# Between two attentions of one network: normalisation split by image, weight products moved, and products of ones at other waits

## Chip, cores and metric

The kernel runs on one core of a Trainium2 chip. The metric is the device time of one execution in microseconds (us); the median over the runs is compared. The engines are TensorE (PE), VectorE (DVE), ScalarE (ACT), GpSimd (POOL) and SyncE (SP), each with a queue of its own that runs in program order and waits on semaphores.

## What is computed

The input is x, two images of 128 channels and 32 x 32 places. Three blocks follow one another.

```python
# 1: attention over 7 x 7 neighbourhoods, on group-normed x
q, k, v = (einsum('bchw,oc->bohw', gn(x), w) + b for each of wq, wk, wv)
frac = einsum('bchw,bcphw->bhwp', q, unfold(k)); attn = softmax(where(frac != 0, frac, -inf))
out = einsum('bhwp,bcphw->bchw', attn, unfold(v))
out = (out - mean over batch and places) * rsqrt(var + 1e-5) * gamma + beta
x = x + relu(out)
# 2: attention over tokens, 8 heads, on layer-normed tokens t (2, 1024, 128)
q, k, v = reshape(ln(t) @ Wqkv + bqkv, (3, b, n, d, h))
attn = softmax(score over queries, axis=1); av = einsum('bnnh,bnqh->bnqh', attn, v)   # the diagonal
t = t + reshape(av) @ W0 + b0
# 3: a mixture of experts, the best 2 of 8 per image, on layer-normed tokens
t = t + ffn(ln(t))            # router on the mean token, gelu, a layer norm at its end
```

All matrix products whose precision matters are made of a rounded part and a remainder (hi and lo), three products in place of one.

## The kernel before, in words

Channels lie on the 128 partitions, the 2048 tokens (image 0, then image 1) on the free axis, in four chunks of 512. PSUM has eight banks of 512 float32; `bank(n)` is one of them and `slot(n)` two neighbouring ones, so the token attention has four slots. All work is written as one list per engine, in program order.

**First attention.** 16 tiles of 128 queries in `CONV_STEPS` steps, software pipelined: scores of tile s, transposes of tile s-2 (L865) into `out_bank`, a copy `probsT` by ACT (L547), products with the values of tile s-3 (L874), and an eviction to `conv_e` by ACT (L562). PE makes products of ones (`keep_warm(bank, count)`, L751: bf16, 128 x 512, result unused) in some of its waits here and later on. DVE then takes batch statistics (L1257, L1316), ACT the square root (L585), DVE scale and bias (L1319 to L1322), ACT six Relus over thirds of an image (L591), and DVE adds x (L1332) and gives x1.

**The fold.** The values' part of the token attention uses W0 folded into the weights: `fold` = 24 blocks of 128 x 128, made from transposed blocks of Wqkv and from W0. PE transposes the 24 blocks (L887), ACT copies them out (L574), PE multiplies (`fold_products`, L905) into six banks, ACT copies those to `fold` (L580). The bias columns go through W0 too (L894), are split into three bf16 parts by POOL (L441, L444), transposed by PE (L956) and copied by DVE (L1362).

**Normalisation of tokens.** `channel_means` (L910, float32 products with 1/128, two instructions for a chunk), `centre` by DVE (L1337), `square` by ACT (L598), `variances` (L918, eight instructions for a chunk), one `root` by ACT (L604), one reciprocal by DVE (L1343), `spread` (L929, eight instructions for a chunk) and the product of both by DVE (L1350) give xn. `LN_PARTS` says which chunks share one root; for the first of the three normalisations all four do. `centred` lies in the same memory as `queries_full`'s two chunks and two more.

**Token attention.** 16 units (image, head), each with one projection of queries and of keys (L981) and eight score tiles (L997 to L999), taken by DVE (`maximum`: L1380 and L1385) and ACT (the exponential with its sum, L644). `JOBS` lists projections, score tiles and one transposition in order; job g lies in slot g % 4 and PE waits in `slot_free(g)` until job g-4 has been taken. A projection of unit u+1 comes behind score tile 0 of unit u; ACT takes hi parts (L622, L634), DVE and POOL the remainders (L1370, L449). The tokens that the reshape gives to image 0's queries are 0 to 341, to its keys 682 to 1024, and to the values 1365 to 2047.

```python
JOBS = [("queries", 0, 0), ("keys", 0, 0)] + [job for u in range(UNITS) for job in unit_jobs(u)]
def job_slot(job):
    return JOB_AT[job] % SLOTS
```

After it come the values (L1047, L1056), the second normalisation, the router, and the experts: `hidden(n)` (L1127 to L1129) and `outputs(n)` (L1142 to L1144) in turn on PE, Gelu on ACT (L724, L731), then the last normalisation and the stores.

Inputs come on SP's and ACT's DMA queues: x in two orders, then Wqkv, W0, x and the experts' weights.

## Time and profile before

| what | value |
|---|---|
| median of 3 runs | 435.48 us (434.71 to 436.42) |
| the profiled execution | 432.75 us |
| its span, first to last instruction | 431.0 us |
| mean granted clock of TensorE | 0.987 of full |
| PE busy | 408.3 us, 95% |
| DVE busy | 322.6 us, 75% |
| ACT busy | 300.2 us, 70% |
| POOL busy | 69.1 us, 16% |

The times of the trace are those of the one profiled execution, so sums are made against its 432.75 us. A busy share is a mean over stages: the last eviction of the first attention starts at 57.60, the first score tile at 90.51, and the last at about 321 us. PE's clock has two levels, 1.2 and 2.4 GHz, shown as 0.50 and 1.00.

### The profile page before, as it was taken

The numbers are of one execution on the slowest core, as the hardware profiler recorded it, in microseconds if no ns is written. First come the engines' busy times: TensorE is split into PE (matmuls) and PEld (weight loads), VectorE is DVE, ScalarE is ACT, GpSimd is POOL, SyncE is SP. The second block draws the span as 40 slices with busy tenths as digits, with TensorE's granted clock in tenths as the row PEclk, the third lists the DMA queues.
The fourth block names the chain that finished last, engine by engine and source line by source line (L and its number), as shares of the span: only waits on it lengthen the run. The fifth ranks groups of instructions, "written<-read, shape, count | busy, mean of one in ns | idle before, by whom it ended". The sixth has DMA issues, their size and how long they took to land.

```text
span 431.0 us, 5798 instructions
## 1 busy us (share of the span) xinstructions
PE 408.3 (95%) x2003; PEld 312.6 (73%) x2007; DVE 322.6 (75%) x707; ACT 300.2 (70%) x579; POOL 69.1 (16%) x72
## 2 busy tenths in 40 slices
PE   7899779999999999999998999999999999879996
PEld 3578766958888888888876888888867666537763
DVE  3788853349888988898899789888997565567654
ACT  1567694459999999999979899999981101555740
POOL 8400011024210221022102112211200000440000
PEclk9999998999999999999999999999999999998998
DMA  7950000000000000000000000000000000000002
GB/s 269 361 144 1 2 2 0 2 0 3 0 1 2 0 2 1 1 2 0 0 2 2 2 0 0 2 1 1 2 0 2 0 0 2 0 2 2 0 2 97
DMA packets 3887, 9.73 MB, mean 23 GB/s; under 512 B 530, under 2 KB 1682, under 8 KB 3730
## 3 DMA queue, kind: packets, MB, share of 16 engines
q1 hardware_dynamic: 3426, 8.39, 5.5%
q10 hardware_dynamic: 432, 0.97, 0.6%
q8 instruction: 16, 0.26, 0.2%
q14 instruction: 13, 0.11, 0.1%
HBM read 8.31 MB, written 1.05 MB: 22 GB/s over the span
## 4 chain that ended last, share of the span: by engine, by line
PE 77%; DVE 14%; ACT 4%; issue 3%; POOLq 0%; POOL 0%; DVEq 0%; ACTq 0%
PE ps L981 12%; PE ps L997 11%; PE ps L999 11%; PE ps L998 11%; PE ps L1056 7%; DVE nmax_all L1380 6%; PE ps L918 3%; PE ps L929 3%; PE ps L751 2%; PE ps L910 2%; PE ps L874 2%; PE ps L1047 1%; PE ps L905 1%; PE ps L849 1%; PE ps L1142 1%
## 5 line engine op out<-in xcount | busy, mean ns | idle before, releaser
L1380 DVE TENSOR_REDUCE nmax_all<-ps 128x1 f32<-128x1024 f32 x128 | 156.8, 1225 | 5.7 <-PE ps L999 3.8
L644 ACT ACTIVATE exps<-ps,nmax_all 128x1024 bf16<-128x1024 f32 x128 | 143.5, 1132 | 13.9 <-DVE diag_all L1385 13.9
L997 PE MATMUL ps<-qT_hi,kT_hi 128*128 128x512 f32 x256 | 104.1, 407 | 2.2 <-ACT exps L644 1.0
L999 PE MATMUL ps<-qT_hi,kT_lo 128*128 128x512 f32 x256 | 99.8, 390 | 0.0
L998 PE MATMUL ps<-qT_lo,kT_hi 128*128 128x512 f32 x256 | 99.7, 389 | 0.0
L449 POOL TENSOR_TENSOR qT_lo<-xq,qT_hi 128x1024 fp32r<-128x1024 f32 x16 | 38.5, 2405 | 198.9 <-ACT xq L634 198.9
L997 PEld LDWEIGHTS ps<-qT_hi,kT_hi 128*128 128x128 f32 x256 | 48.1, 188 | 14.9 <-ACT exps L644 2.0
L981 PE MATMUL ps<-xn,wqkv 128*128 128x342 f32 (+3 forms) x256 | 58.2, 379 | 0.0
L998 PEld LDWEIGHTS ps<-qT_lo,kT_hi 128*128 128x128 f32 x256 | 48.1, 188 | 10.8
L999 PEld LDWEIGHTS ps<-qT_hi,kT_lo 128*128 128x128 f32 x256 | 48.1, 188 | 10.3
L981 PEld LDWEIGHTS ps<-xn,wqkv 128*128 128x128 f32 x256 | 42.6, 189 | 10.9 <-ACT exps L644 0.5
L1370 DVE SCALAR_TENSOR_TENSOR kT_lo<-ps,cols,kT_hi 128x341 fp32r<-128x341 f32 (+1 forms) x48 | 24.5, 567 | 30.8 <-ACT kT_hi L622 30.8
L1385 DVE CUSTOM_DVE_ANT_0 diag_junk<-ps,ident 128x128 f32<-128x128 f32 x128 | 36.0, 281 | 0.0
L1056 PE MATMUL ps<-xs,fold 128*128 128x342 f32 (+3 forms) x128 | 30.6, 381 | 0.6 <-DVE xs L1446 0.6
L622 ACT ACTIVATE kT_hi<-ps,cols 128x341 fp32r<-128x341 f32 (+1 forms) x48 | 22.7, 546 | 10.5 <-PE ps L981 10.5
L598 ACT ACTIVATE squares<-xq 128x512 f32<-128x512 f32 x12 | 7.5, 629 | 29.9 <-DVE xq L1337 29.9
L1446 DVE TENSOR_TENSOR xs<-xv,ps 128x1024 f32<-128x1024 f32 x16 | 19.4, 1220 | 11.2 <-PE ps L1047 11.2
L644 ACT ACTIVATION_READ_ACCUMULATOR exps<-ps,nmax_all 128x1 f32 x128 | 27.7, 217 | 0.0
L751 PE MATMUL ps<-filler 128*128 128x512 bf16 x84 | 23.8, 427 | 2.7 <-DVE filler L1189 1.5
L1056 PEld LDWEIGHTS ps<-xs,fold 128*128 128x128 f32 x128 | 21.1, 189 | 6.6 <-DVE xs L1446 1.1
L634 ACT ACTIVATE qT_hi<-ps,bqkv_q 128x341 fp32r<-128x341 f32 (+1 forms) x48 | 23.0, 570 | 1.4 <-PE ps L981 1.4
L634 ACT ACTIVATE xq<-ps,bqkv_q 128x341 f32<-128x341 f32 (+1 forms) x48 | 23.3, 594 | 0.0
(200 smaller groups left out, 516.4 us busy)
## 6 DMA issues: line engine op xcount, KB each, us to landing
wqkv<-laid_qkv_weights SPq DMA_DIRECT2D x1, 1536.0 KB, 6.2
xq<-laid_x_queries SPq DMA_DIRECT2D x2, 512.0 KB, 6.8
xk<-laid_x_keys SPq DMA_DIRECT2D x2, 512.0 KB, 8.3
x<-in_x SPq DMA_DIRECT2D x1, 1024.0 KB, 9.3
w<-in_L_ffn_W SPq DMA_DIRECT2D x1, 1024.0 KB
out<-conv_e SPq DMA_DIRECT2D x4, 256.0 KB, 2.0
band_sb<-laid_band ACTq DMA_DIRECT2D x1, 724.0 KB, 10.0
w<-in_L_attn_W SPq DMA_DIRECT2D x1, 512.0 KB, 7.2
```

The costliest lines, as they stand in the source:

```text
L449: g.tensor_tensor(qT_lo[:, u % 2, :], queries_full, qT_hi[:, u % 2, :].bitcast(F32), ALU.subtract)\
L634: a.activation(dst[:, lo:hi], slot(job_slot(("queries", u, 0)), lo, hi), ACT.Identity, bias=bqkv_q[:, j, h:h + 1], scale=SCORE_SCALE).then ...
L644: a.activation(exps[:, n % 2, :], slot(job_slot(("score", u, n))), ACT.Exp, bias=nmax_all[:, col:col + 1], accum_out=sum_all[:, col:col + ...
L751: mm(bank(n), filler[:, 0:P], filler[:, :], start=True, stop=True)
L981: last = mm(slot(job_slot((kind, u, 0)), at, at + n), wqkv[:, h, j, :], xn[:, tok:tok + n], start=True, stop=True)
L997: mm(tgt, keys_hi, qT_hi[:, u % 2, at], start=True, stop=False)
L998: mm(tgt, keys_hi, qT_lo[:, u % 2, at], start=False, stop=False)
L999: last = mm(tgt, keys_lo, qT_hi[:, u % 2, at], start=False, stop=True)
L1056: last = mm(slot(SUMS_SLOT[b], at, at + n), fold[:, h, j, :], xs[:, u % 2, at:at + n], start=False, stop=False, skip_group_check=True)
L1370: inst = v.scalar_tensor_tensor(kT_lo[:, u % 2, lo:hi], slot(job_slot(("keys", u, 0)), lo, hi), bqkv[:, j, h:h + 1], kT_hi[:, u % 2, lo:hi ...
L1380: v.tensor_reduce(nmax_all[:, col:col + 1], slot(place), AX_X, ALU.max, negate=True)\
L1385: v.tensor_tensor_reduce(out=diag_junk[:, :], in0=slot(place, tile * P, (tile + 1) * P), in1=ident[:, :], scale=1.0, scalar=0.0, op0=ALU.m ...
```

## The change

- **By DMA.** Transposed blocks of Wqkv come as an input of their own (`qkv_weights_T`, 1.5 MB) into `wvT`, in memory that is used otherwise only during the token attention. The 24 transposes and their six copies are gone. The new transfer is issued behind Wqkv and ahead of W0, x and the rest.
- **The fold's place.** The bias products come first behind the first attention's last product, in bank 0, then all six banks of fold products (banks 6, 7, 1, 2, 6, 7), ahead of the channel means. ACT copies banks 0 and 1 of them before the square root of the batch statistics, and the others behind the Relus.
- **Batch statistics.** The addition of 1e-5 goes into the root's bias, a product and a subtraction become one instruction. The Sqrt table is loaded in step 16 of the first attention's 19 and not behind it. ACT makes the Relus of image 0 only; POOL scales and shifts the thirds of image 1, and DVE takes their maximum with 0 in the same instruction that adds x.
- **Normalisation in two parts**, chunks 0 and 1 (one root) and chunks 2 and 3. Only chunks 0 and 1 are finished before the first projection. The spread of chunks 2 and 3 and their two products become a job in unit 1 ahead of score tile 4, the transposition of the bias parts one in unit 2 ahead of tile 4. With two more jobs, the slots and banks of the value stage, the second normalisation and the router are renumbered. POOL's copy of the values' tokens goes one unit later.
- **Products of ones.** Removed: one ahead of the first group statistics, one behind them. Added or moved: 11 at four waits behind the fold; 3, 5 and 7 (5, 5 and 5 before) around the first evictions; 12 between the first hidden products and the first outputs; 3 ahead of the last three spreads; and 4 and 4 with a wait between where 14 stood ahead of the last spread.

```diff
-        FOLD_AT = (5, 7, 6, 5, 7, 6)
+        FOLD_AT = (6, 7, 1, 2, 6, 7)
+        VB_BANK = 0
...
-        LN_PARTS = [((0, 1, 2, 3),), ((0, 1), (2, 3)), ((0, 1, 2), (3,))]
+        LN_PARTS = [((0, 1), (2, 3)), ((0, 1), (2, 3)), ((0, 1, 2), (3,))]
...
+        EXTRA_AT = {"spread": (1, 4), "biases": (2, 4), "turned": (HEADS + 1, 4)}
...
+            sp.dma_start(wvT[:, :, :, :], t["qkv_weights_T"]).then_inc(wvT_in, 16)
...
+            pool.wait_ge(bn_aff, 1)
+            pool.wait_ge(folded, 2)
+            for lo, hi, _ in THIRDS:
+                third = conv_e[:, 1, lo * RUN:hi * RUN]
+                g.tensor_scalar(third, third, st[:, 30:31], st[:, 31:32], ALU.mult, ALU.add).then_inc(bn_scaled, 1)
...
                     take_job(*STEP_JOB[s])
-
-            load_table(ACT.Sqrt)
...
-            take_transposed(0, 2)
-
-            act.wait_ge(bn_eps, 1)
-            a.activation(st[:, 26:27], st[:, 26:27], ACT.Sqrt).then_inc(bn_root, 1)
-            take_transposed(2, 4)
+                if s == CONV_TILES:
+                    load_table(ACT.Sqrt)
...
+            take_folded(0)
+            take_folded(1)
+            act.wait_ge(bn_stats, 1)
+            a.activation(st[:, 26:27], st[:, 25:26], ACT.Sqrt, bias=norm_eps[:, :]).then_inc(bn_root, 1)
             act.wait_ge(bn_aff, 1)
             act.wait_ge(folded, 2)
-            for b in range(2):
-                for lo, hi, _ in THIRDS:
-                    a.activation(conv_e[:, b, lo * RUN:hi * RUN], conv_e[:, b, lo * RUN:hi * RUN], ACT.Relu,
-                                 scale=st[:, 30:31], bias=st[:, 31:32]).then_inc(bn_relu, 1)
-            take_transposed(4, FOLD_BANKS)
+            for lo, hi, _ in THIRDS:
+                third = conv_e[:, 0, lo * RUN:hi * RUN]
+                a.activation(third, third, ACT.Relu, scale=st[:, 30:31], bias=st[:, 31:32]).then_inc(bn_relu, 1)
+            for n in range(2, FOLD_BANKS):
+                take_folded(n)
...
-            for c in range(4):
-                square(0, c)
-            take_folded(0, 2)
             act.wait_ge(norm_consts, 3)
-            root(0, 0, 4)
+            square(0, 0)
+            square(0, 1)
+            root(0, 0, 7)
+            square(0, 2)
+            square(0, 3)
+            root(0, 1, 0)
             load_table(ACT.Exp)
-            take_folded(2, FOLD_BANKS)
...
             pe.wait_ge(xq_in[0], 16)
-            keep_warm(7, 4)
+            keep_warm(7, 3)
...
+            pe.wait_ge(wvT_in, 16)
+            for job in (("q", 2 * CHUNKS - 1), ("v", 2 * CHUNKS - 1)):
+                taken(*job)
+            for n in range(FOLD_BANKS):
+                fold_products(n)
+            for signal, count, times in ((bn_root, 1, 3), (bn_aff, 1, 3), (bn_relu, 1, 3), (bn_relu, 2, 2)):
+                pe.wait_ge(signal, count)
+                keep_warm(5, times)
...
+            pe.wait_ge(cx_sb, CONV_TILES)
+            pe.wait_ge(x1_ready, 3)
+            channel_means(0, 0, x1, "mean", 3)
+            channel_means(0, 1, x1, "mean", 4)
+            pe.wait_ge(x1_ready, 6)
+            channel_means(0, 2, x1, "mean", 5)
+            pe.wait_ge(f_m_sb, 5)
+            channel_means(0, 3, x1, "mean", 6)
+            pe.wait_ge(f_m_sb, 6)
+            variances(0, 0, 7, 0)
+            variances(0, 0, 7, 1)
+            pe.wait_ge(vb_sb, 1)
+            variances(0, 1, 0, 2)
+            variances(0, 1, 0, 3)
+            pe.wait_ge(LN[0]["centred"], 2)
+            spread(0, 0, 3)
+            spread(0, 1, 4)
+            pe.wait_ge(LN[0]["sqrt"], 2)
...
+            def spread_rest(n):
+
+                pe.wait_ge(LN[0]["rstd"], 2)
+                for i in range(8, 16):
+                    last = mm(bank(n + i // 4 - 2, i % 4 * P, (i % 4 + 1) * P), row_sel[:, i, :], rstd[:, 1, :],
+                              start=True, stop=True)
+                last.then_inc(job_ps, 1)
...
+                    if (u, n) == EXTRA_AT["spread"]:
+                        dve.wait_ge(job_ps, JOB_AT["spread", 0, 0] + 1)
+                        place = 2 * job_slot(("spread", 0, 0))
+                        for c in (2, 3):
+                            at = slice(c * 512, (c + 1) * 512)
+                            v.tensor_tensor(xn[:, at], centred[:, at], bank(place + c - 2), ALU.mult)\
+                                .then_inc(LN[0]["out"], 1)
...
             hidden(0)
             hidden(1)
+            keep_warm(7, 8)
+            pe.wait_ge(h_sb, 1)
+            keep_warm(7, 4)
...
+            keep_warm(5, 3)
             for c in range(3):
                 spread(2, c, 1 + c)
             pe.wait_ge(u_ready, 4)
             variances(2, 1, 6, 3)
-            keep_warm(5, 14)
+            keep_warm(5, 4)
+            pe.wait_ge(LN[2]["sqrt"], 2)
+            keep_warm(5, 4)
             spread(2, 3, 4)
```

## Rows read from the trace of the kernel before

**Rows 1.** Chain that ended last: start us, us, engine and line.

```profile
1.52 6.39 PE ps L751 x16
...
61.04 1.68 PE ps L894 x16
62.72 1.60 issue
64.32 5.37 PE ps L910 x8
...
90.51 0.50 PE ps L997
```

**Rows 2.** Timeline in the second normalisation: start us, us, engine, line, operation, count.

```profile
365.18 1.88 PE L910 MATMUL ps<-t,mean_w 128*128 128x512 f32 x4
...
367.71 1.92 PE L918 MATMUL ps<-squares,mean_window 128*16 128x128 f32 x16 [0.65 <-ACT squares L598]
```

**Rows 3.** Timeline of PE, first expert outputs; in brackets the idle time before.

```profile
388.84 0.47 PE L1142 MATMUL ps<-hid_hi,w_hi 128*128 128x512 f32 x1 [2.03 <-ACT hid_hi L731]
...
393.26 0.40 PE L1142 MATMUL ps<-hid_hi,w_hi 128*128 128x512 f32 x1
```

**Rows 4.** Windows of PE: from:to, length, busy (count), granted clock, DMA, GB/s.

```profile
65.50:66.00 0.50, 0.50 (x2) 0.50 0.00 0
...
389.50:390.00 0.50, 0.50 (x3) 0.50 0.00 0
...
420.50:421.00 0.50, 0.50 (x4) 0.50 0.19 74
```

**Rows 5.** Timeline of PE in the first attention.

```profile
48.78 0.41 PE L865 MATMUL ps<-ident,probs 128*128 128x128 f32 x2 [1.95 <-DVE probs L1294]
```

**Rows 6.** Chain that ended last, projections in the token attention.

```profile
92.16 3.46 PE ps L981 x16
106.53 3.46 PE ps L981 x16
```

**Rows 7.** Group of the page: busy us, mean ns of one, idle before.

```profile
L1380 DVE TENSOR_REDUCE nmax_all<-ps 128x1 f32<-128x1024 f32 x128 | 156.8, 1225 | 5.7 <-PE ps L999 3.8
```

**Rows 8.** Timeline of ACT at the end of the first attention.

```profile
55.71 0.48 ACT L562 ACTIVATE conv_e<-ps,conv_b 128x128 f32<-128x128 f32 x1 [0.19 <-PE ps L874]
56.04 0.48 ACT L547 COPY probsT<-ps 128x384 f32<-128x384 f32 x1
...
57.60 0.48 ACT L562 ACTIVATE conv_e<-ps,conv_b 128x128 f32<-128x128 f32 x1 [0.41 <-PE ps L874]
58.10 1.28 ACT L497 ACT_TABLE_LOAD   x1
...
59.51 1.06 ACT L574 COPY xv<-ps 128x512 f32<-128x512 f32 x2
60.45 0.21 ACT L585 ACTIVATE st<-st 128x1 f32<-128x1 f32 x1
...
61.50 3.50 ACT L591 ACTIVATE conv_e<-conv_e,st 128x352 f32<-128x352 f32 x6
```

**Rows 9.** Timeline of PE in the first normalisation: fold, first projections.

```profile
69.53 1.95 PE L905 MATMUL ps<-w,xv 128*128 128x128 f32 x16
...
82.80 3.68 PE L981 MATMUL ps<-xn,wqkv 128*128 128x342 f32 x16
```

**Rows 10.** Timeline of POOL at the start.

```profile
15.96 0.48 POOL L430 TENSOR_SCALAR conv_ws<-conv_wT,st 128x256 f32<-128x256 f32 x1 [0.92 <-DVE st L1206]
```

**Rows 11.** Timeline at the end of the kernel.

```profile
422.42 3.55 PE L751 MATMUL ps<-filler 128*128 128x512 bf16 x13 [0.33 <-issue]
422.68 0.93 DVE L1343 RECIPROCAL rstd<-rstd 16x128 f32<-16x128 f32 x1
...
427.09 0.69 DVE L1350 TENSOR_TENSOR xq<-xq,ps 128x512 f32<-128x512 f32 x1 [3.48 <-PE ps L929]
```

**Rows 12.** Slices of the page, 40 over the span: busy tenths of the DMA engines.

```profile
DMA  7950000000000000000000000000000000000002
```

224 lines of the change are left out of this document (109 added, 115 removed).

## Prediction

> **What bounds the kernel now.** I read the chain that ended last first, because TensorE (PE) is busy nearly everywhere and the busy share alone says little. Three places matter. Between the attentions [rows 1] the chain is PE: products of bias columns from 61.04, 1.60 us in which PE does nothing, four channel means from 64.32 that take 5.37 us, then folds, variances and spreads up to the first projection, and the first score tile at 90.51. The reader should see that the means are 8 instructions of 0.67 us each, while the same 512 column means later take 0.47 (four in 1.88) [rows 2]. The windows by clock say why: at 65.5 the granted clock is 0.50, the 1.2 GHz level, right after the idle 1.60 us. The same level stands at 389.5, after 2.03 us of idle PE [rows 3], and at 420.5 near the end [rows 4]. But 1.95 us of idle PE before 48.78 in the first attention was followed by no fall [rows 5], so idle time alone does not decide it.
>
> The long stretch of score tiles is PE's too: 14.37 us from one unit's projections to the next [rows 6], of which 3.46 are projections and 8 tiles take 1.36 each. VectorE (DVE) takes 1.23 for a maximum [rows 7], and the picking of the diagonal fills the tile's time up, so it keeps step in the tiles and catches up only during the projections: 3.46 less the key remainders over 1024 elements, which I put at 1.5 (an estimate: a maximum reads as many in 1.23, and these are three starts), so 1.9 us per unit.
>
> **Start.** One product of ones fewer before the group statistics. The chain begins with these 16 products [rows 1], not with the statistics, so one product comes off the path: 512 columns at 2.4 GHz, 0.213 us. The other one removed lies ahead of a wait for scaled weights: nothing. Sum: -0.2.
>
> **The Sqrt table.** Its load moves from behind the last eviction of the first attention to two steps earlier, behind the eviction at 55.71. There ScalarE (ACT) has no free time: the copy of the last transposed tile started at 56.04 [rows 8], overlapping that eviction, which ends at 56.19. The load costs 1.41 from its start to that of the next instruction (58.10 to 59.51), so the copy starts at about 57.60, 1.56 late, and with it PE's last three products, the last eviction and the statistics. Before, that load lay beside the statistics, so nothing is gained for it. The Trainium skill ("ScalarE: Activation LUTs", What ACT_TABLE_LOAD costs) adds a drain of about 1.38 us to the 1.28 of each load; the trace shows 1.28 and the next instruction 0.13 behind it. By that rule the step would be 1.25 dearer; I take the row.
>
> **PE's queue from there.** The 24 transposes and their six copies go, since the transposed weights come by DMA. PE ended the last product by 57.60, where its eviction starts [rows 8]; now 59.15. The 16 bias instructions take 1.7 to 1.85 (1.68 in the chain, 62.72 the end) [rows 1] and end at about 60.9. The six fold banks follow at once: 24 blocks of two instructions. Sixteen took 1.95 with the tail of the last [rows 9], 0.1175 a step, so 48 take 5.64, to 66.6. Banks 6 and 7 are used twice, for which ACT must have copied the first two; it has. Then 11 products of ones at four waits, 0.213 each: 2.35 us, to 68.9. They are not free unless the waits are late, so check them. The square root waits behind the copy of the second bank on ACT: that bank ends at 62.8 and its copy takes 0.53 (two in 1.06), so the root starts at 63.4. From the root's start to the first Relu were 1.05 with four steps of DVE; with three, 0.9: 64.3 instead of 61.50 [rows 8], 2.8 later although the statistics are ready 1.56 late only. Three Relus of 0.58 (six in 3.50) end at 66.0, the sums of image 0 at 66.5 and, three of about 0.45 more, of image 1 at 67.9. All four waits are thus over before PE comes to the products of ones, and PE's queue sets the means: 68.9.
>
> Image 1's thirds go to GpSimd (POOL). The nearest row is 0.48 for 256 elements [rows 10]; a third has up to 352, so 0.6 to 0.7 each, ready at 66.4, needed by the third mean at 70.6. Cover 4 us.
>
> **Normalisation.** Four means at full clock, 0.86 each, end at 72.4. From a mean's start to the variance of its square are 2.53 [rows 2], long over by then, so PE goes on with the variances of chunks 0 and 1, 16 steps, to 74.3. ACT takes the root before square 2: with 0.4 for the root and 0.7 for the square (an estimate: 2.53 less a mean, shared by centring and square, leaves 0.8) PE idles 1.1, then variances 2 and 3 to 77.3. Two spreads, 1.9, end at 79.2. The reciprocal (0.93) [rows 11] is long done. Queries need chunk 0 only, keys chunk 1. So the projection starts at 79.2 instead of 82.80 [rows 9], and from projection to first score (90.51) is the same chain of evictions, 7.7 us: first score at 86.9. The products of ones in it lie beside evictions. Between the attentions: -3.6.
>
> **What is given back.** The spread of chunks 2 and 3 (16 instructions, 1.88) and the three bias transposes (three steps, 0.35) stand now among the score tiles, where PE is the bound: +2.2. DVE gets two products of 0.69 (as in [rows 11]) behind a maximum, and one small copy. The spread's own slot is freed by those two; the score tile four jobs on waits some 0.3 for it: +0.3. The rest of DVE's delay is under the 1.9 of the next projections. Sum: +2.5.
>
> **Feed-forward.** Twelve products of ones now fill the idle 2.03. They take 2.56, start where PE fell idle (386.65 by the step, 388.84 less 2.03 less the tail) and end at 389.2, 0.35 past the old start. Twelve products from 388.84 to 393.26 took 4.42 [rows 3]; at full clock twelve take 2.76 (a score tile's six take 1.36, and a little for the join). Gain 1.66 less 0.35 = 1.3, of which I take 1.2, since the Gelu chain is close behind.
>
> **End.** Before, 14 products of ones stand between the last variance and the last spread, part of them at half clock: 422.42 to 425.97 [rows 11]. The reciprocal starts at 422.68, behind the third chunk's output on DVE, and is done at 423.6. With eight split by a wait the spread starts at 423.7 when the clock stays up, and the last normalisation at 424.85 for 427.09: -2.2. When the clock still falls, the eight end near 424.6: -1.3. The three new ones before the spreads lie where PE waits for a reciprocal. I take 2.1, near the full-clock end, since these three fill idle time right ahead of the fall.
>
> **DMA.** The 1.5 MB more is queued on SyncE ahead of W0, x and the feed-forward weights. All inputs are over within the first three slices of 10.8 us, where the DMA share of a slice falls from 9 tenths to 5 and then to nothing [rows 12]; the 1.5 MB, a sixth more than what was moved in all, reach about half a slice further, and the transposed weights, W0 and x are first used at 59 or later. Nothing. The value stage only exchanges banks: nothing.
>
> **Sum.** -0.2 - 3.6 + 2.5 - 1.2 - 2.1 = -4.6. The profiled execution took 432.75 (span 431.0): 428.15, span 426.4. The median of the runs is 2.73 above the profiled time, so 435.48 - 4.6 = 430.9.
>
> **Rivals.**
> *The clock falls in the fold.* The table load opens 1.56 us of idle PE, after which come six short products and 1.85 us of three-column products, the make-up that preceded the fall at 65.5 [rows 1, 4]; against it stands the gap before 48.78 without one [rows 5]. One stretch at half clock cost 1.66 in the feed-forward [rows 3]; 1.7: 432.6. Chance 0.27.
> *The products of ones don't hold the clock* in the feed-forward (then they only cost 0.35, so 1.55 worse) or at the end (0.8 worse): up to 433.2. For it: the fall at 420.5 stood behind spreads with no long idle time. Chance 0.14.
> *The table load is hidden*, since the copy is not as tight as in this execution: 1.56 better, 429.3. Against it: the start of 56.04 lies inside the previous eviction [rows 8]. Chance 0.08.
> *POOL holds image 1 (the other side).* If a third took over 1.9 us instead of 0.6, the means of image 1 wait; at 4.2 us each the gain of 4.6 and 2.2 more are gone: over 437.7. It decides from 3.4 us on. The row of 0.48 for 256 elements speaks against it. The Trainium skill ("SBUF — State Buffer", Who interferes with whom) lets a DVE instruction with two SBUF inputs and a GpSimd one that reads SBUF block each other for a whole instruction. By that rule POOL would wait for up to three sums of 0.45, some 1.4 more, still covered; no row here shows such a pair. Chance 0.03.
> *DVE's delay in the attention is not absorbed*: another 1.4, 432.3. Chance 0.06, in no sum of the others.
>
> **Numbers.** My forecast 0.42. Range 428.6 (table hidden, a little more) to 433.5 (half clock, or ones without effect). About 0.5% (2.2 us) is what a measurement of this kernel can tell from no change. Faster by more needs under 433.3: forecast, hidden load, most of the two clock rivals, 0.84; within, 0.12; slower, 0.04.
>
> **What would show it.** The last copy of probsT 1.5 after the eviction before it. The four means right behind the products of ones, at 0.43 per instruction and clock 1.00. The first projection near 79, the first score near 87. One unit longer by 2.2 and 0.3, another by only 0.35. Clock 1.00 at 389 to 393. No PE gap of more than 0.9 before the last spread. It would be wrong if PE waited for a sum of image 1, if the half clock stood in 58 to 66, or if score tiles waited for slots for more than 0.5 us.

## The result and the profile after

The change makes the kernel faster: a median of 430.55 us over 20 runs (428.15 to 435.86) beside 434.25 (432.76 to 436.42, 20 runs) of the kernel before, ratio 0.9909, 95% interval 0.9884 to 0.9934. The ratio leaves out four runs of the changed kernel (435.09 to 435.86) that lie more than 1.5% above its fastest; the medians keep them. The forecast of 430.9 stood on a median of 435.48 from 3 runs; over 20 runs that median is 434.25, so the medians fell by 3.70 and not by 4.6, and the near hit on 430.55 is in part luck. The profiled execution took 428.15 (span 426.4, mean granted clock 0.999), 4.60 less than the one of before.

Stage by stage, each cut at the first instruction of a step, from the two profiled executions:

| stretch, us | before | after | difference | predicted |
|---|---|---|---|---|
| start of the span to the first score product of the first attention | 15.78 | 14.62 | -1.16 | -0.2 |
| from there to the first score tile of the second | 74.73 | 70.88 | -3.85 | -3.6 |
| from there to the first `xs` of the values | 231.86 | 235.48 | +3.62 | +2.5 |
| to the first hidden product | 61.37 | 61.38 | 0.0 | 0 |
| to the start of the last outputs | 29.53 | 28.32 | -1.21 | -1.2 |
| to the last normalisation | 13.82 | 11.80 | -2.02 | -2.1 |

The sum came out as predicted, -4.6, but because two terms missed in opposite directions: the start is 1.0 better and the attention 1.1 worse than the prediction had them. The start's 1.0 is luck of this pair of executions, as the last part of this section shows.

**Between the attentions.** The chain that ended last; it answers to [rows 1] and the fold and projections of [rows 9]:

```profile
57.05 0.91 PE ps L871 x6
57.96 1.68 PE ps L884 x16
59.64 5.46 PE ps L892 x48
65.10 2.37 PE ps L748 x11
67.48 3.43 PE ps L906 x8
70.91 1.86 PE ps L914 x16
...
73.82 1.91 PE ps L914 x16
75.73 1.98 PE ps L925 x16
...
77.79 1.98 PE ps L973 x8
...
85.50 0.50 PE ps L989
```

The 1.60 us of idle PE and the slow means are gone. PE goes from the last products of the first attention through the bias products (L884), the 48 fold instructions (L892), 11 products of ones (L748) and the means (L906) without a wait, and the eight mean instructions take 3.43 for 5.37.

The timeline of ACT at the end of the first attention, beside [rows 8]:

```profile
54.55 0.48 ACT L563 ACTIVATE conv_e<-ps,conv_b 128x128 f32<-128x128 f32 x1 [0.19 <-PE ps L871]
55.04 1.28 ACT L498 ACT_TABLE_LOAD   x1
...
56.45 0.46 ACT L548 COPY probsT<-ps 128x384 f32<-128x384 f32 x1
```

and PE behind it:

```profile
57.05 0.91 PE L871 MATMUL ps<-probsT,vtok 128*128 128x128 f32 x6 [1.55 <-ACT probsT L548]
```

The load starts right behind an eviction, and the last transposed tile is copied 1.41 later; PE waits 1.55 for it.

The batch normalisation and the first sums, on three engines:

```profile
63.10 1.80 ACT L585 ACTIVATE conv_e<-conv_e,st 128x352 f32<-128x352 f32 x3 [0.75 <-DVE st L1347]
63.17 3.11 POOL L438 TENSOR_SCALAR conv_e<-conv_e,st 128x352 f32<-128x352 f32 x3 [46.89 <-DVE st L1347]
63.88 1.63 DVE L1360 TENSOR_TENSOR x<-x,conv_e 128x352 f32<-128x352 f32 x3 [0.72 <-ACT conv_e L585]
...
65.43 1.62 DVE L1363 SCALAR_TENSOR_TENSOR x<-conv_e,x 128x352 f32<-128x352 f32 x3
```

POOL's thirds take 1.04 each in the mean (one by one 0.63, 0.95 and 1.55), and DVE's sums of image 1 follow 1.55 behind those of image 0. All are over at 67.05, before the first mean at 67.48.

**In the attention.** Chain, projections, and the spread's job (L1008), beside [rows 6]:

```profile
87.15 3.46 PE ps L973 x16
...
101.52 3.46 PE ps L973 x16
...
109.08 1.98 PE ps L1008 x16
...
126.74 0.50 PE ps L989
...
133.85 3.46 PE ps L973 x16
```

From the projections at 101.52 to those at 133.85 (two units, the middle ones start at 118.22) are 32.33 us where two plain units take 28.74: 3.59 more, all that the attention lost. In the second of these units PE waits 0.53 for an exponential (L641) ahead of the tile at 126.74.

**Feed-forward and end.** Timelines of PE, beside [rows 3] and [rows 11]:

```profile
385.26 2.76 PE L748 MATMUL ps<-filler 128*128 128x512 bf16 x12
387.68 0.58 PE L1161 MATMUL ps<-hid_hi,w_hi 128*128 128x512 f32 x1
...
418.80 1.90 PE L748 MATMUL ps<-filler 128*128 128x512 bf16 x8
...
421.29 1.15 PE L925 MATMUL ps<-rstd,row_sel 16*128 16x128 f32 x8 [0.59 <-DVE rstd L1373]
```

The outputs follow the products of ones without a gap. At the end the reciprocal starts at 420.30 and takes 0.93, as in [rows 11], but the spread waits 0.59 for it and not for a row of fourteen products. Windows of PE where the clock was at half in [rows 4] (length, busy, count, granted clock):

```profile
65.50:66.00 0.50, 0.50 (x4) 1.00 0.00 0
389.50:390.00 0.50, 0.50 (x4) 1.00 0.12 33
420.50:421.00 0.50, 0.20 (x1) 1.00 0.13 45
```

**The start.** Timeline of DVE and POOL of the kernel before:

```profile
9.21 3.56 POOL L416 TENSOR_SCALAR_AFFINE_SELECT head_sel<-head_sel 72x1024 bf16<-72x1024 bf16 x3
...
9.71 1.90 DVE L1224 TENSOR_SCALAR conv_ws<-conv_wT,st 128x128 f32<-128x128 f32 x3
```

and after:

```profile
8.93 1.51 DVE L1249 TENSOR_SCALAR conv_ws<-conv_wT,st 128x128 f32<-128x128 f32 x3
9.19 3.64 POOL L412 TENSOR_SCALAR_AFFINE_SELECT head_sel<-head_sel 72x1024 bf16<-72x1024 bf16 x3
```

DVE's three scalings of the convolution's weights started 0.78 earlier and ended 1.17 earlier (10.44 for 11.61). The three selects take 1.09 to 1.18 each and start 1.23 to 1.32 apart. After, the scalings end 0.08 behind POOL's first select (10.36), before, 0.08 behind its second (11.53). The prediction did not look at this pair.

The 0.78 is not the removed product alone. At the start the products of ones begin 0.43 us apart, and at some moment they go over to 0.21. That moment differs between executions, and with it the time at which PE comes to the statistics. Two of the experiments below, e9 and e10, have the changed kernel's instructions up to here. Their timelines, e9:

```profile
1.52 5.14 PE L748 MATMUL ps<-filler 128*128 128x512 bf16 x15 [1.52 <-DVE filler L1211]
...
8.56 0.83 DVE L1246 TENSOR_SCALAR conv_ws<-conv_wT,st 128x128 f32<-128x128 f32 x3
```

and e10:

```profile
1.52 6.35 PE L748 MATMUL ps<-filler 128*128 128x512 bf16 x15 [1.52 <-DVE filler L1211]
...
9.66 1.92 DVE L1246 TENSOR_SCALAR conv_ws<-conv_wT,st 128x128 f32<-128x128 f32 x3
```

The same 15 products take 5.14, 5.62 (changed kernel) and 6.35 us; the 16 of before took 6.39 [rows 1]. Over all profiled executions that have the selects at the start:

| profiled executions | first scaling starts (first select: 9.19 to 9.21) | statistics of image 1 start |
|---|---|---|
| e2, e3, e6, e8, e9 | 8.56 to 8.67 | 10.05 to 10.37 |
| changed kernel, e7 | 8.93, 8.89 | 10.49, 10.45 |
| e1 (16 products of ones) | 9.23 | 11.64 |
| e4, e5, e10 | 9.34, 9.61, 9.66 | 11.64 |
| kernel before (16 products of ones) | 9.71 | 11.66 |

An execution whose scalings start ahead of the select starts the statistics of image 1 some 1.2 us earlier, and three of the ten executions with 15 products did not get that far.

### The profile page after: what moved, and what is told of

The parts are those of the page before. It is cut to its first block, busy times and chain, and to the rows that moved or that the text cites. A ratio compares the mean times of both kernels' runs of the same rounds, so it can differ in the third digit from the quotient of the medians.

```text
span 426.4 us, 5791 instructions
## 1 busy us (share of the span) xinstructions
PE 405.3 (95%) x2001; PEld 308.8 (72%) x2001; DVE 323.1 (76%) x707; ACT 295.5 (69%) x571; POOL 71.4 (17%) x75
## 4 chain that ended last, share of the span: by engine, by line
PE 73%; DVE 17%; ACT 6%; issue 3%; POOLq 0%; POOL 0%; DVEq 0%; ACTq 0%
PE ps L973 11%; PE ps L989 10%; PE ps L991 10%; PE ps L990 10%; DVE nmax_all L1414 7%; PE ps L1075 7%; PE ps L748 3%; PE ps L914 2%; PE ps L906 2%; PE ps L925 2%; PE ps L871 2%; PE ps L1066 1%; PE ps L846 1%; PE ps L892 1%; ACT exps L641 1%
## 5 line engine op out<-in xcount | busy, mean ns | idle before, releaser
L641 ACT ACTIVATE exps<-ps,nmax_all 128x1024 bf16<-128x1024 f32 x128 | 143.3, 1132 | 18.5 <-DVE diag_all L1419 17.9
L748 PE MATMUL ps<-filler 128*128 128x512 bf16 x106 | 27.9, 405 | 2.2 <-DVE filler L1214 1.5
L641 ACT ACTIVATION_READ_ACCUMULATOR exps<-ps,nmax_all 128x1 f32 x128 | 27.9, 218 | 0.0
```

What stands on the lines that cost most here:

```text
L641: a.activation(exps[:, n % 2, :], slot(job_slot(("score", u, n))), ACT.Exp, bias=nmax_all[:, col:col + 1], accum_out=sum_all[:, col:col + ...
L748: mm(bank(n), filler[:, 0:P], filler[:, :], start=True, stop=True)
```

## The experiments

Each profiled execution has its own stretches at half clock (of about 4 us at the fold, 4 to 11 us in the router between 366 and 390, and at the end), so a step is compared with the same step at the same clock.

**e1: the start put back.**

```diff
-            keep_warm(7, 3)
+            keep_warm(7, 4)
...
-            keep_warm(7, 2)
+            keep_warm(7, 3)
```

> The changed kernel with the two products of ones at the start restored (4 and 3 in place of 3 and 2). In the two traces everything behind the start was 1.16 us earlier with the change, where the prediction had 0.2. Theory: the two products are worth that 1.16, the first by its own 0.4 (it runs at the low start rate) and the rest by what lies beside it on GpSimd, so the first score product of the first attention goes back from 14.6 to about 15.8. Rival: the 0.2 of the prediction is right and the rest is the landing of the first input, which differs from execution to execution (DVE began its first statistics at 5.47 before and at 5.01 after); then that product starts at about 14.8 to 15.2, whatever the products of ones.

Measured (one run, 433.91): the first score product at 15.76 for 14.62 (15.78 before). In this execution the fold fell to half clock, 7.09 us for 5.46; less that, the stretch up to the second attention is the changed kernel's to 0.01 (72.51 less 1.63, and 70.88). The timeline of e1:

```profile
9.19 3.55 POOL L412 TENSOR_SCALAR_AFFINE_SELECT head_sel<-head_sel 72x1024 bf16<-72x1024 bf16 x3
9.23 2.36 DVE L1249 TENSOR_SCALAR conv_ws<-conv_wT,st 128x128 f32<-128x128 f32 x3
```

DVE starts 0.04 behind POOL and not 0.26 ahead, and its three take 2.36: the first ends with the first select (10.36), the second in the gap before the next, the third with the second select (11.59). The first product at 15.76 is what the theory had, but one run does not show that the products of ones are its cause: e4, e5 and e10 lose the same race without them. In e1's own execution one product fewer, 0.21, would have put the scalings at 9.02, ahead of the select (an estimate); in that of the kernel before, at 9.50, it would not. The rival, a later landing of the input, fell: DVE's first statistics start at 4.89 here for 5.01.

**e11: POOL's selects away from DVE's scalings.** The memset and the selects of `head_sel` go behind the remainder of the first queries; PE waits for them before the first broadcast.

```diff
-            step(g.memset(head_sel[:, :, :], 0.0))
-            for part in range(3):
...
+            pool.wait_ge(ws_ready[0], 3)
             g.memset(conv_e[:, :, :], 0.0).then_inc(zeroed, 1)
...
                 queries_remainder(u)
+                if u == 0:
+                    step(g.memset(head_sel[:, :, :], 0.0))
```

> The changed kernel with GpSimd's memset and its three selects of head_sel moved from the start to behind the remainder of the first queries, and the memset of conv_e behind VectorE's three scalings of the convolution's weights: GpSimd is idle while VectorE scales. Theory (VectorE's scalings are held by GpSimd's selects): the three take 0.72 us in all for 1.51, each in 0.24, and the first score product is at 13.8 for 14.62. Rival (the scalings wait for something else, or the second image's landing is late next): the three still take 1.5, or they take 0.72 and the first score product stays at 14.6. The selects, now at some 82 to 87 us, may hold VectorE there by up to 1 us ahead of the first exponentials.

Measured: 428.85 (4 runs), ratio 0.9859 (0.9816 to 0.9902). Its timeline:

```profile
8.61 0.68 DVE L1250 TENSOR_SCALAR conv_ws<-conv_wT,st 128x128 f32<-128x128 f32 x3
...
10.25 1.29 DVE L1222 BATCH_NORM_STATS2 bn<-xq 128x6 f32<-128x512 f32 x2 [0.53 <-DMA xq<-laid_x_queries]
```

With POOL's selects away, three scalings take 0.68 for 1.51, 1.90 and 2.36: it was POOL that held them. The first score product comes at 14.39, only 0.23 earlier, because now the landing of the second half of `xq` at 10.23 is late: DVE's statistics wait 0.53 for it. Both halves of the expectation are thus answered, the hold by the theory, the gain by the rival; in the changed kernel the statistics start at 10.49, so its start has 0.25 left to give, and kernels that won the race with the selects in place (e3, e6) are at 14.27 and 14.19. What the move buys is that the race cannot be lost.

**e2: the table load back behind the last eviction.**

```diff
-                if s == CONV_TILES:
-                    load_table(ACT.Sqrt)
+
+            load_table(ACT.Sqrt)
```

> The changed kernel with the Sqrt table loaded behind the loop of the first attention again. Theory (the prediction's term): the load in step 16 holds the copy of the last transposed tile and with it PE's whole queue by 1.56 us, so without it the gap of 1.55 us in PE before the last products goes, and the first score tile of the token attention starts 1.5 us earlier, 84.0 for 85.5 where the start is the same; the time falls by 1.5 us. Rival: the load then lies in the way of the fold's first copies and of the root, and the gain is taken back there: under 0.3 us, or a loss.

Measured: 428.40 (4 runs), ratio 0.9878 (0.9816 to 0.9940). From the first score product to the second attention 69.35 for 70.88: 1.53 less. The bias products start at 56.28 for 57.96, without a gap ahead of PE's last products, and all behind them follows in the same distances (fold 5.46, products of ones 2.37, means 3.43), since PE's queue sets the time. The early load bought nothing and cost what the prediction had for it (1.56).

**e3: without the 11 products of ones behind the fold.**

```diff
-            for signal, count, times in ((bn_root, 1, 3), (bn_aff, 1, 3), (bn_relu, 1, 3), (bn_relu, 2, 2)):
-                pe.wait_ge(signal, count)
-                keep_warm(5, times)
```

> The changed kernel without the 11 products of ones between the fold and the channel means. Theory (the prediction's term): all four waits are over when PE comes to them, so they cost 2.3 us and hold nothing; the sums of image 0 are ready at 65.5 and those of image 1 at 67.05, the fold ends at 65.1, so the means start at 65.5 for 67.5 and PE then waits for the second image's sums once, a few tenths: the first score tile comes 1.7 to 2.0 us earlier. Rival: the products keep the clock up, and without them the means run at 1.2 GHz as in the kernel before: then the gain of 2 is eaten by 1.7 and the time stays the same within 0.5 us.

Measured: 429.96 (10 runs), ratio 0.9870 (0.9834 to 0.9905); the interval overlaps the changed kernel's. The profiled execution has the fold at half clock, as e1's has; against e1 the stretch is 71.17 for 72.51, 1.34 less and not 2.37, since PE now waits for image 0's sums. Its chain:

```profile
65.40 1.65 DVE x L1357 x3
67.05 0.14 issue
67.18 3.67 PE ps L903 x8
```

The means ran at full clock behind that wait, so these 11 products did not hold the clock here. Of their 2.37 us 1.34 come back in this execution. The sums are late in it because the root stands behind ACT's copy of the second fold bank, which the half clock delays (its copy starts at 63.09, the root at 63.57). At whole clock, as in the changed kernel's trace, image 0's sums are over at 65.51, so 1.97 would come back (an estimate: 67.48 less 65.51); and with the root ahead of those copies 2.19 do (e9 against e2, 67.16 for 69.35, both at whole clock there).

**e4: the spread's job ahead of the next unit's projections, at tile 1 of unit 1.**

```diff
-        EXTRA_AT = {"spread": (1, 4), "biases": (2, 4), "turned": (HEADS + 1, 4)}
+        EXTRA_AT = {"spread": (1, 1), "biases": (2, 4), "turned": (HEADS + 1, 4)}
```

and in the order of jobs it stands ahead of the keys and queries, with DVE's two products ahead of the tile's maximum.

> The changed kernel with the spread of chunks 2 and 3 as the job ahead of the projections in unit 1 (behind score tile 0), and its two products on DVE ahead of the key remainders. Theory: of the 3.6 us that units 1 and 2 take more than two others, 1.98 and 0.35 are PE's own work and 1.26 come from DVE, whose two products of 0.69 stand where it keeps step with PE; behind score tile 0 DVE waits 1.7 us for key remainders anyway, so they are free there, and units 1 and 2 together take 31.1 us in place of 32.3, the time falls by 1.2. Rival: the 1.26 are a wait for the slot that the spread holds, wherever it stands: units 1 and 2 keep 32.3 and the time is the same.

Measured: 436.24 (10 runs), ratio 0.9947 (0.9902 to 0.9993). From the first score tile of the second attention to `xs` 235.97 for 235.48. The theory fell: DVE has the projections to catch up in, and the attention still loses as much. (The rest of the 10.0 us that this profiled execution takes more than the changed kernel's is the lost race at the start, 1.2, and half clock: 2.8 more at the start, 2.5 up to the second attention, 2.1 in the router, 0.9 at the end.) The timeline of PE shows where:

```profile
107.93 2.05 PE L1010 MATMUL ps<-rstd,row_sel 16*128 16x128 f32 x16
...
114.51 0.50 PE L991 MATMUL ps<-qT_hi,kT_hi 128*128 128x512 f32 x1 [0.87 <-ACT exps L643]
```

The wait is not one for DVE. The tile behind the projections (109.91, 3.73 long) waits for an exponential on ACT, which stands behind the eviction of the keys. That speaks for the rival, a cost of the extra job wherever it stands; e7 and e10 test it.

**e7: the second half's spread and products in the wait for the first keys.** The job in the attention stays, with one product of ones of 128 columns in it.

```diff
             pe.wait_ge(LN[0]["centred"], 4)
-            keep_warm(5, 3)
-            pe.wait_ge(q_full, 2)
-            keep_warm(5, 5)
+            spread(0, 2, 5)
+            spread(0, 3, 6)
             pe.wait_ge(k_hi, 2)
-            keep_warm(5, 7)
+            keep_warm(7, 7)
+            pe.wait_ge(LN[0]["out"], 3)
...
+            normalise(0, 2, 5, xn)
             keys_remainder(0)
+            normalise(0, 3, 6, xn)
...
-                for i in range(8, 16):
-                    last = mm(bank(n + i // 4 - 2, i % 4 * P, (i % 4 + 1) * P), row_sel[:, i, :], rstd[:, 1, :],
-                              start=True, stop=True)
+                mm(bank(n, 0, P), filler[:, 0:P], filler[:, 0:P], start=True, stop=True).then_inc(job_ps, 1)
```

> The changed kernel with the spread of chunks 2 and 3 in the place of 8 products of ones behind the first two projections, where PE waits for evictions, and DVE's two products on both sides of the first key remainders; the job in unit 1 is one product of ones without a use. Theory: both are free there, so the first score tile stays at 70.9 us behind the first attention's first score and the stretch from it to the values falls from 235.5 to 232.4 (the bias job with its slot and copy is left), 3 us faster. Rival: the excess comes from the two extra jobs in the ring of four slots and not from the work in them: then it falls by PE's 1.9 only.

Measured: 429.75 (4 runs), ratio 0.9873 (0.9780 to 0.9966). The first score tile comes at 85.53 (85.50): the work in the wait is free. The attention is 233.41 for 235.48: 2.07 less, and not the 3 of the theory: the rival held. The spread's own time (1.98) came back, with 0.09 beside it for all of DVE's two products, and 1.55 of the loss stayed with two jobs, of which one holds a single short product and the other the three transposes.

**e9: all moves together.** e7 and the bias transposes in the same wait (their job empty too), the table load of e2, no products of ones behind the fold (e3), and the root of the batch statistics ahead of the copies of the first two fold banks.

```diff
+            act.wait_ge(bn_stats, 1)
+            a.activation(st[:, 26:27], st[:, 25:26], ACT.Sqrt, bias=norm_eps[:, :]).then_inc(bn_root, 1)
             take_folded(0)
             take_folded(1)
-            act.wait_ge(bn_stats, 1)
-            a.activation(st[:, 26:27], st[:, 25:26], ACT.Sqrt, bias=norm_eps[:, :]).then_inc(bn_root, 1)
```

> All that the runs point to: as the one before, with the bias transposes in that wait as well, the Sqrt table loaded behind the loop, the root ahead of the fold's first two copies and no products of ones ahead of the means. Theory: 1.5 for the table, 2 for the products, 3.3 for the work taken out of the score tiles: the first score tile at 81.5 to 82.5, the values' first product at 314, 6.5 us faster than the changed kernel in the same state of the clock. Rival: once the fold's end comes earlier, the sums of the second image are late next, GpSimd's three thirds of 1.04 us each behind the root, and PE falls idle ahead of the means so that the clock falls there: 3 to 4 us faster only.

Measured: 423.09 (4 runs), ratio 0.9737 (0.9683 to 0.9790). First score tile at 81.67, where the theory had it, and the rival did not come: PE does not wait ahead of the means, and the clock stays whole there. From the first score product to `xs` e9 is 5.8 shorter than the changed kernel and not 6.5, since the attention keeps 233.43: emptying the second job changed nothing (233.41 in e7). Its timeline of PE at the first of the two jobs:

```profile
104.86 0.39 PE L988 MATMUL ps<-qT_hi,kT_lo 128*128 128x512 f32 x1
105.09 0.23 PE L1003 MATMUL ps<-filler 128*128 128x128 bf16 x1
105.72 0.50 PE L986 MATMUL ps<-qT_hi,kT_hi 128*128 128x512 f32 x1 [0.40 <-ACT exps L641]
```

One product of 128 columns, then 0.40 us of wait for an exponential; the unit, from the projections at 97.52 to those at 112.66, is 15.14 long for 14.37. The job has taken a place in the ring of four, so the tile behind it needs the slot of the tile three before it, not four.

**e10: e9 without the two jobs.** 161 jobs, slots and banks of the later stages as in the kernel before.

```diff
-        EXTRA_AT = {"spread": (1, 4), "biases": (2, 4), "turned": (HEADS + 1, 4)}
+        EXTRA_AT = {"turned": (HEADS + 1, 4)}
-        SUMS_SLOT = (3, 2)
+        SUMS_SLOT = (1, 0)
```

> The kernel that has all moves ahead of the attention (e9), and without its two extra jobs, which there held one product of ones each: 161 jobs in the ring of four as before the change, with the slots of the sums and of the broadcasts and the banks of the second normalisation as before. Theory (an extra job costs the ring some 0.8 whatever is in it): from the second attention's first score tile to the xs of the first values product 231.9 us for 233.4, and the span 1.5 less where the clock is the same. Rival (the 1.6 that is left comes from the order ahead of the jobs, the first unit's keys and queries): the stretch stays at 233.4.

Measured: the attention takes 231.82 for 233.43 (231.86 before the change): the theory held, 0.8 for each job. The chain has the plain distance again, also across the units that held them:

```profile
85.67 3.46 PE ps L970 x16
...
100.05 3.46 PE ps L970 x16
...
128.79 3.46 PE ps L970 x16
```

The median of 424.06 (6 runs, ratio 0.9766, 0.9732 to 0.9800) doesn't show it beside e9's 423.09; the intervals overlap. The profiled execution has its first score product at 16.88, 2.37 behind e9's: 1.27 of that is the lost race of the scalings (statistics of image 1 at 11.64 for 10.37), and 1.10 a stretch at half clock from 10.5 to 14.5. Why the clock falls there in some executions stays open.

**e6: all four chunks finished ahead of the first projections.** The jobs stay, each with its one short product or its transposes.

```diff
+            pe.wait_ge(LN[0]["centred"], 4)
+            spread(0, 2, 5)
+            spread(0, 3, 6)
             pe.wait_ge(LN[0]["sqrt"], 2)
+            pe.wait_ge(LN[0]["out"], 4)
```

> The changed kernel with all four chunks spread and finished ahead of the first projections; the spread's job in unit 1 is one product of ones without a use, so that all slots stay. Theory: the first score tile comes 1.9 later (two spreads on PE), the stretch from it to the values loses 1.9 of spread, 0.35 of slot wait and about 0.5 to 0.9 of DVE backlog, so the split by image is a loss of about 1 us where it stands: 1 us faster than the changed kernel. Rival: the split is what makes the change faster; without it the time is 2 us longer.

Measured: 434.32 (10 runs), ratio 0.9954 (0.9917 to 0.9992). From the means to the first score tile 24.62 for 18.19; in this execution 2.9 of the 6.4 are half clock (the spreads 3.28 for 1.98, the first projections 3.57 for 1.98), which leaves some 3.5 (an estimate) that the split is worth there. The attention takes 233.40, 2.08 less than the changed kernel. The theory, that the split is a loss of 1 us, fell: the split gains more than it gives back, by some 1.4 us, not by its whole size.

**e5 and e8: start, feed-forward and end.** e5 is the kernel before with the products of ones of these three places as changed:

```diff
             hidden(0)
             hidden(1)
+            keep_warm(7, 8)
+            pe.wait_ge(h_sb, 1)
+            keep_warm(7, 4)
...
+            keep_warm(5, 3)
...
-            keep_warm(5, 14)
+            keep_warm(5, 4)
+            pe.wait_ge(LN[2]["sqrt"], 2)
+            keep_warm(5, 4)
```

> The kernel before with the change's products of ones only: 3 and 2 at the start, 12 in the feed-forward, 3 and then 4 and 4 at the end. Theory: these are worth 1.16 at the start (DVE's weight scaling then begins ahead of GpSimd's selects at 9.19), 1.2 in the feed-forward and 2.0 at the end, 4.4 in all, so the time is that of the changed kernel within 1 us: the rest of the change is worth nothing net. Rival: the gain of the changed kernel comes from the stretch between the attentions, and the products of ones alone give under 2 us.

Measured: 434.54 (10 runs), ratio 0.9977 (0.9945 to 1.0009). From the hidden products to the last outputs 28.38 (29.53 before, 28.32 after). The end 12.72 (13.82 and 11.80): here the clock fell at 423.5 all the same, and the chain has the last variances (0.98 for eight at full clock) and the products of ones at half clock:

```profile
424.32 1.82 PE ps L918 x8
426.14 2.39 PE ps L751 x8
```

The gain of the two places, 2.2 in this execution, was lost to stretches at half clock elsewhere: the start (10.5 to 14.5, the first score product at 16.88 for 15.78; the scalings start at 9.61, behind the select, and end at 11.59 for 11.61, so the removed products gave nothing), a second one between the attentions (82.5 to 86, 76.37 for 74.73) and the router (63.43 for 61.37). The theory, 4.4 us from the products of ones alone, fell, and the rival held: by the medians (434.54 beside 434.87) they give 0.3 us, and this interval doesn't tell the ratio from 1. The two terms are there in their stages, and less than their sum is left in the whole.

e8 is the changed kernel with the same two places of the feed-forward and the end as before.

> The changed kernel with the products of ones ahead of the outputs and around the last spread put back as they were before (none at the outputs, 14 in one piece at the end). Theory (the prediction's steps): both stretches lengthen to what they were: from the hidden products to the last outputs 29.5 us for 28.32, from there to the last normalisation 13.8 for 11.80, so 3.2 in all, everything ahead of the outputs as it is. Rival (both gains are the clock's, which falls at other places in other executions): either stretch stays within 0.3 of the changed kernel's wherever the granted clock is whole.

Measured: 432.98 (10 runs), ratio 0.9964 (0.9935 to 0.9994). The two stretches are 29.40 and 13.85, as the theory had them to 0.1, and the half clock is back at 391.5 and 422.5. Of all profiled executions only this one and the kernel before, the two without the twelve products ahead of the outputs, show the clock falling between the hidden products and the last outputs; the twelve with them don't. At the end the products hold less: with them the clock stays up in four (11.80) and falls in eight (12.72 to 12.82). Windows of e8 (length; busy and count of PE, PEld, DVE, ACT and POOL; then the granted clock):

```profile
391.50:392.00 0.50, 0.50 (x2) 0.33 (x1) 0.46 (x3) 0.00 (x0) 0.00 (x0) 0.50 0.00 0
422.50:423.00 0.50, 0.50 (x2) 0.15 (x1) 0.47 (x2) 0.30 (x1) 0.00 (x0) 0.50 0.10 33
```

**e12: e10 and e11 together.**

> The two edits of e10 and e11 together. Theory: both gains add up: a span of some 419 us at a whole clock in the fold and the router, about 2.3 less than e9's 421.2. Rival: the selects beside the first unit's keys take back what the start gave, and the span is that of e10.

Measured: 422.35 (6 runs, 421.39 to 423.66), ratio 0.9725 (0.9692 to 0.9757), the fastest of all, 11.9 below the 434.25 of before and 8.2 below the changed kernel's median. The profiled span is 419.9, 1.3 below e9's. That is less than the 2.3 of the theory: the attention gave its 1.6 (231.82) and the start only 0.04 (14.47 for 14.51), while by the clock the router was 0.7 shorter and the end 1.0 longer (12.82 for 11.80). The selects beside the first keys cost nothing that is seen: the first score tile is at 81.66 (81.67).

## Why the prediction was right, point by point

- **Start (-0.2; measured -1.16): mis-sized, and the larger part is luck.** The step priced the product of ones at 0.213 us, the pace of full clock, where its own row has 16 in 6.39 [rows 1], and the sum let the whole chain behind it follow. What lay behind it was a race between DVE's scalings and POOL's selects, worth some 1.2 us according to who comes first (e11, and the table of starts above). In this pair of executions the race was won because the products of ones reached their faster pace earlier (15 in 5.62, 16 in 6.39), and one product fewer would not have done it in the execution of before (9.50, an estimate, and the select at 9.21). e5, the kernel before with 15, gained 0.02 at the end of the scalings. The sign stood in the trace of before: three scalings in 1.90 beside POOL's selects, 0.63 each in the mean, where POOL itself took 0.48 for twice the elements [rows 10]. The Trainium skill ("SBUF — State Buffer", Who interferes with whom) describes this hold: it names `tensor_scalar` among the DVE instructions that can take the port pair shared with GpSimd, and says that whoever issues first keeps the pair for its whole instruction and the other blocks. The prediction applied that section to POOL's thirds only. The traces agree: in the changed kernel the two scalings that start ahead of the select (8.93, 9.14) take under 0.3 each, the third, which starts within it, ends 0.08 behind it, and without the selects all three are over in 0.68.
- **Table load (+1.56).** Right: PE waits 1.55, and e2 gives 1.53 back. From the load's start are 1.30 to the one-column instruction that comes with it and 1.41 to the copy behind that, in [rows 8] and again here; the drain of 1.38 on top of 1.28 that the Trainium skill has ("ScalarE: Activation LUTs", What ACT_TABLE_LOAD costs) is not seen, though the load stood right behind an eviction here. The rival of a hidden load is out with that.
- **PE's queue (bias products to means 68.9).** Right in its order: 1.68, 5.46 for 5.64, 2.37 for 2.35; the means start at 67.48, which is 68.9 less the start's 1.16 and 0.3. All four waits were over. It was also right that the early table load and the products of ones are costs and not cover: e2 and e3 without them are 1.53 and 1.34 shorter there.
- **POOL's thirds (0.6 to 0.7; measured 1.04 in the mean).** Right for a third by itself and too low for the three, covered as predicted. In e9 they are over before DVE's sums begin and take 0.62 each:

```profile
59.43 1.83 POOL L438 TENSOR_SCALAR conv_e<-conv_e,st 128x352 f32<-128x352 f32 x3 [43.19 <-DVE st L1344]
```

Beside the sums they take 0.63, 0.95 and 1.55, in all 1.3 longer, near the 1.4 that the prediction allowed for this hold in its rival. That rival needed 3.4 us a third to undo the gain.

- **Normalisation.** The idle time ahead of the second variances was 1.06 for 1.1, from the first projection to the first score 7.71 for 7.7. The first score tile is at 85.50 for 86.9, of which 1.16 is the start.
- **What is given back (+2.5; measured +3.62): mis-sized.** The failing step is "the score tile four jobs on waits some 0.3 for it", with the 0.35 of the transposes taken as the whole price of their job: 0.65 for what the two jobs cost beside the spread's work, where 1.55 were measured (e7). That "the rest of DVE's delay is under the 1.9 of the next projections" was right. The spread's products cost 1.98 to 2.07 (e7), as predicted. What was missing is 0.8 for each of two jobs whatever is in them (e7, e9, e10): an extra job takes a slot of the ring of four, and a tile behind it waits for an exponential that in the plain order would have been over (0.40 of the 0.77 in e9; the rest is the job's own product and the starts around it). The price of the transposes and that of the wait are not to be added: with and without them the stretch is the same (233.41, 233.43), so they lie in the wait. The rival that DVE's delay is not absorbed is out: e7 takes DVE's two products away with the spread and gains only 0.09 beyond the spread's 1.98. The prediction's own sign, a tile waiting over 0.5 for its slot, is just met (0.53 at 126.74).
- **Feed-forward (-1.2; -1.21) and end (-2.1; -2.02).** Right; e8 undoes both terms (+1.08, +2.05), and e5 shows that with the clock fallen at the end 1.1 of the 2.0 is left, near the 1.3 that the prediction gave for this case. That is the commoner case: eight of the twelve profiled executions with these products end so. That the changed kernel's own had the whole 2.0 is luck.
- **DMA (nothing).** Right: the DMA share of the third slice is 8 tenths for 5 [rows 12], and then nothing as before.
- **The clock in the fold (the first rival).** Not in the profiled execution of the changed kernel, whose clock is whole, but in others: of the eight kernels with the table load early, six show the fold at half clock in their profiled execution (the changed kernel and e7 don't), at 1.63 where the chain shows it (7.09 for 5.46); of the four with the load at its old place (e2, e9, e10, e12), none does. The rival's price, 1.7, was right, and its cause, the gap that the load opens, is supported by these counts and not proven by them. The kernel before with its idle 1.60 us fell too, in both of its traces (e5's is the other). It fits that the changed kernel's median lies 2.40 above its profiled time (2.73 was carried over from the kernel before): the profiled execution, at a whole clock, is the fastest of the 20.
- **The products of ones don't hold the clock (the second rival).** In the feed-forward they do, at the end in four of twelve; behind the fold they are not needed (e3, and e9, e10 and e12, where the clock is whole without them). The prediction counted their 2.35 as the change's cost, rightly.

## What to carry to other kernels

Price a step that is put into a full ring by its place in the ring first and by its work second: here an empty job cost 0.8 us, and the same work in a wait ahead of the ring cost nothing. Before pricing a product or a wait that is removed, look which instructions of other engines start shortly behind it: who came first of DVE and POOL was worth 1.2 us, five times the product. Then ask whether the removal decides that order or the execution does: the same instructions won it in seven traces and lost it in three. One trace before and one after can't tell the two apart. And move a table load only to where its engine has idle time; a load beside work that nobody waits for is free where it is.

## What the runs showed of the hardware

- Three DVE scalings of 128x128 from SBUF to SBUF took 0.68, 1.51, 1.90 and 2.36 us, with POOL's selects absent, starting 0.26 behind them, 0.50 ahead of them and 0.04 ahead of them, and 0.83 with the selects 0.63 behind (e9). The order of the 1.90 and the 2.36 is by where in a select of 1.09 us the first scaling falls.
- Three POOL scalings of 128x352 took 1.83 us by themselves (e9) and 3.11 beside DVE's sums with two SBUF inputs, whose middle one took 0.72 for 0.53 and 0.50.
- The same 15 products of ones at the start took from 5.04 (e11) to 6.35 us (e10): they begin 0.43 apart and then 0.21 apart, and the change comes at 4.9 us in one execution and behind 7.4 in another.
- One and the same kernel took from 428.15 to 435.86 us, with a mean granted clock of 0.999 and 0.976. Which stretches ran at half clock is known of profiled executions only. In the router that alone is 0.9 (e8) to 3.7 us (e3) beside the 61.38 of the changed kernel: the 24 products of ones there took 8.13 us in e1 and were not on the chain at all in the changed kernel's own execution:

```profile
379.33 8.13 PE ps L748 x24
```

- The stretch 10.5 to 14.5 us ran at half clock in the profiled executions of e5 and e10, and in e4 on to 20.5. It costs 1.1 us in e10. The three are those with 15 products of ones that lost the race of the scalings; e1 and the kernel before lost it too and did not fall. This window of e10 shows it; its cause was not found:

```profile
12.00:12.50 0.50, 0.50 (x3) 0.50 0.38 147
```
